# A macaron model's experts stage: the copy of the turned routing weights ahead of the update r, and the transposes of r one unit later

## What is computed

```python
x = x + 0.5 * _L0_ffn_ref(_layernorm(x, axis=-1), ...)
x = x + _L0_attn_ref(_layernorm(x, axis=-1), ...)
x = x + 0.5 * _L0_ffn_ref(_layernorm(x, axis=-1), ...)
x = x + 0.5 * _L1_ffn_ref(_layernorm(x, axis=-1), ...)   # experts, first call
x = x + _L1_attn_ref(_layernorm(x, axis=-1), ...)
x = x + 0.5 * _L1_ffn_ref(_layernorm(x, axis=-1), ...)   # experts, second call
```

```python
xn = (x - mu) * jax.lax.rsqrt(var + EPS) * ln_gamma + ln_beta
abel_out = _gelu(xn @ abel_w + abel_b)
logits = xn @ moe_gate_w + moe_gate_b
topw, topi = jax.lax.top_k(logits, K)
topw = jax.nn.softmax(topw, axis=-1)
w_dense = jnp.sum(jax.nn.one_hot(topi, E, dtype=xn.dtype) * topw[..., None], axis=-2)
h = _gelu(jnp.einsum('bsd,edh->ebsh', xn, ew1) + eb1[:, None, None, :])
eo = jnp.einsum('ebsh,ehd->ebsd', h, ew2) + eb2[:, None, None, :]
moe_out = jnp.einsum('ebsd,bse->bsd', eo, w_dense)
for i in range(NROT):
    moe_out = moe_out @ expm(gens[i])
combined = jnp.concatenate([abel_out, moe_out], axis=-1)
gate = jax.nn.sigmoid(combined @ gc_w + gc_b)
mixed = abel_out * (1.0 - gate) + moe_out * gate
return residual + mixed
```

## Time and profile before

| what | value |
|---|---|
| median of 3 runs | 1009.28 us |
| lowest and highest | 1007.32 and 1010.31 us |
| the profiled execution | 1007.76 us |
| its span in the trace | 1006.0 us |
| PE busy | 859.9 us |
| DVE busy | 711.1 us |
| ACT busy | 638.6 us |
| POOL busy | 604.4 us |
| unit-by-unit work of call one, first product of unit 0 to the last unit's | 313 to 529 us |
| the same of call two | 779 to 992 us |

### The profile page before, as it was taken

The page is one execution under the profiler, slowest core; times in us unless marked ns, Lnnn a source line. Parts: engine busy times, 40 slices in busy tenths (PEclk is TensorE's granted clock), DMA queues, the critical chain, the costliest instruction groups (busy, mean ns, idle before and its releaser), DMA issues.

```text
span 1006.0 us, 14102 instructions
## 1 busy us (share of the span) xinstructions
PE 859.9 (85%) x3862; PEld 460.3 (46%) x3862; DVE 711.1 (71%) x1535; ACT 638.6 (63%) x1153; POOL 604.4 (60%) x610
## 2 busy tenths in 40 slices
PE   7879677767975999999996688888886899999997
PEld 6734333354432444444443355555543344444443
DVE  6945469965563878887863277777786787887774
ACT  3167489967755887778783444444322787778884
POOL 2064675667458766666675254444457766667674
PEclk9999788869997999999997799999997999999999
DMA  8000000000002222211120000000000213223320
GB/s 213 11 1 0 0 0 1 1 1 1 1 0 85 84 86 85 79 48 58 69 84 0 1 1 0 1 1 1 1 1 1 101 69 95 94 94 95 94 95 22
DMA packets 27406, 42.10 MB, mean 42 GB/s; under 512 B 5320, under 2 KB 19036, under 8 KB 27356
## 3 DMA queue, kind: packets, MB, share of 16 engines
q1 hardware_dynamic: 27356, 41.52, 13.0%
HBM read 39.15 MB, written 2.36 MB: 41 GB/s over the span
## 4 chain that ended last, share of the span: by engine, by line
PE 35%; issue 22%; DVE 19%; POOL 14%; ACT 9%; SPq 1%; DVEq 0%; POOLq 0%; DMA 0%; ACTq 0%
PE bank L1478 7%; PE bank L1480 7%; PE bank L1479 7%; POOL arena L810 5%; POOL arena L754 4%; PE bank L1708 3%; DVE arena L1324 3%; ACT bank L1001 3%; POOL rstd L712 2%; DVE arena L1367 1%; DVE arena L1366 1%; DVE stats L1173 1%; PE bank L1678 1%; ACT arena L993 1%; PE bank L1715 1%
## 5 line engine op out<-in xcount | busy, mean ns | idle before, releaser
L790 POOL TENSOR_TENSOR arena<-arena 128x512 f16<-128x512 f32 x256 | 295.3, 1166 | 125.3 <-ACT arena L993 123.5
L1324 DVE TENSOR_TENSOR arena<-bank,arena 128x512 f32<-128x512 f32 x256 | 172.5, 685 | 79.6 <-ACT bank L1001 63.3
L993 ACT ACTIVATE arena<-arena 128x512 f16<-128x512 f32 x256 | 160.8, 628 | 73.8 <-DVE arena L1324 73.7
L1001 ACT ACTIVATE bank<-bank,eb 128x512 f32<-128x512 f32 x256 | 166.8, 656 | 18.9 <-PE bank L1480 18.5
L817 POOL TENSOR_TENSOR arena<-arena 128x512 f32<-128x512 f32 (+1 forms) x24 | 32.7, 1371 | 117.2 <-DVE arena L1442 89.9
L1478 PE MATMUL bank<-arena,ew1hi 128*128 128x512 f16 x256 | 98.5, 385 | 2.0 <-DVE arena L1324 2.0
L1479 PE MATMUL bank<-arena,ew1hi 128*128 128x512 f16 x256 | 98.5, 385 | 0.0
L1480 PE MATMUL bank<-arena,ew1lo 128*128 128x512 f16 x256 | 97.9, 382 | 0.0
L1478 PE MATMUL bank<-arena,ew2hi 128*128 128x512 f16 x256 | 97.3, 380 | 0.1
L1479 PE MATMUL bank<-arena,ew2hi 128*128 128x512 f16 x256 | 97.3, 380 | 0.0
L1480 PE MATMUL bank<-arena,ew2lo 128*128 128x512 f16 x256 | 97.3, 380 | 0.0
(11 more groups left out here) (274 smaller groups left out, 1876.2 us busy)
## 6 DMA issues: line engine op xcount, KB each, us to landing
arena<-wrows SPq DMA_DIRECT2D x64, 512.0 KB, 5.4
X<-in_L_attn_x_dram SPq DMA_DIRECT2D x8, 256.0 KB, 4.3
out_dram<-X SPq DMA_DIRECT2D x8, 256.0 KB, 6.7
arena<-in_L_ffn_ew_dram SPq DMA_DIRECT2D x2, 512.0 KB, 6.4
arena<-in_L_ffn_ew_dram SPq DMA_DIRECT2D x1, 1024.0 KB
wrows<-arena SPq DMA_DIRECT2D x16, 16.0 KB
arena<-in_L_ffn_gens_dram SPq DMA_DIRECT2D x1, 192.0 KB, 2.7
arena<-in_L_ffn_w_gate_dram SPq DMA_DIRECT2D x1, 192.0 KB, 2.9
```

The lines of the kernel that those rows point to most:

```text
L790: pool.tensor_tensor(mo.hlo[:, u % 8, :], mo.hw[:, u % 4, :], mo.hhi[:, u % 8, :], ALU.subtract).then_inc(S.hlo, 1)
L993: A(mo.hhi[:, u % 8, :], mo.hw[:, u % 4, :], ACT.Copy).then_inc(S.hhi, 1)
L1001: A(bank[MM1_BANK[u]][:, :], bank[MM1_BANK[u]][:, :], ACT.Gelu, scale=1.0 / WS, bias=eb1[:, u:u + 1]).then_inc(S.gelu, 1)
L1324: TT(mo.hw[:, u % 4, :], bank[MM1_BANK[u]][:, :], mo.wB[:, p, u // EB, :], ALU.mult)\
```

## The change

On DVE, the copy wT moves from the end of unit 10 to the place right behind the unit-10 product, ahead of m and r. On PE, the transposes of r move from unit 12 to unit 13, that is behind abel and behind the unit-13 first product and the second product beside it. The addition to X stays where it is. Nothing else is changed; ACT, POOL and SP have the same lists.

```diff
@@ experts, VectorE
+                        if lead and u == 10:
+                            dve.wait_ge(S.wpT, i + 2)
+                            after(dve, S.wd, 16 * i)
+                            dve.tensor_copy(mo.wT[0:E, n, :], bank[7][0:E, :]).then_inc(S.wT, 1)
                         if lag and u == 10:
 
                             dve.wait_ge(S.tg, i)
...
-                        if lead and u == 10:
-                            dve.wait_ge(S.wpT, i + 2)
-                            after(dve, S.wd, 16 * i)
-                            dve.tensor_copy(mo.wT[0:E, n, :], bank[7][0:E, :]).then_inc(S.wT, 1)
                 pipeline(dve, first, NCH, step)
@@ experts, TensorE
-                        if lag and u == 12:
+                        if lag and u == 13:
                             pe.wait_ge(S.r, i)
```

## The result

| | before | changed |
|---|---|---|
| median of 4 runs each | 1009.79 us | 1002.90 us |
| lowest and highest | 1007.32 and 1010.81 us | 1001.92 and 1003.03 us |
| ratio, 95% interval | | 0.9935 (0.9919 to 0.9950) |
| profiled execution, its span | 1007.76, 1006.0 us | 1002.81, 1001.1 us |
| first product of a call to the last transposes of r, both calls | 448.83 us | 441.37 us |

The change is 6.9 us faster in the medians. The forecast was 8.8 us faster, 1000.5 us: right sign, 2.4 us off. The time lies 0.4 us outside the narrower range that was given (998.5 to 1002.5) and inside the wider one (996.5 to 1005.5). The two calls give 7.46 us by the traces.

What follows compares the result with a forecast made beforehand. PE, busy 26.38 us of each 27.2 to 27.3 us step, was held about 0.9 us by r. Terms 0.37 + 5.8 + 1.8 + 0.8 = 8.8 us off 1009.28 gave 1000.5 us; range 998.5 to 1002.5, wider 996.5 to 1005.5.

Steps and rivals of the forecast that it cites:

- first period of call one: First step-to-step period of call one: xn slack at the gate logits only 0.42 us, worth 0.37 us.
- four other steady periods of call one: Call one's part of the nine steady periods, each 0.64 us shorter, capped by PE's wait for xn.
- five steady periods of call two: Call two's part of the nine steady periods, each 0.64 us shorter, capped by PE's wait for xn.
- two periods from step 6 to step 7: No next chunk is led in, so no wait for xn: PE keeps its whole 0.89 us, twice.
- two tails: End of each call: r transposes and last second product wait less, 0.4 us each, bounds 0.1 and 0.45.
- The copy ahead of m and r: On DVE, copy starts about 0.6 us after the unit-10 product; PE waits 0.30 us at abel instead of 1.04.
- The transposes behind unit 13: On PE, they wait for nothing, cost 0.44 us, with 1.5 us of cover before L1210; PE gains 0.89 a step.
- What is late next: Gate logits (L1678) wait for xn: PE comes forward 0.64 us, not 0.89; the other 0.25 becomes a new wait.
- DVE, ACT and POOL keep their order and distance from unit 10 to xn: Argument against the slower rival: these engines' sequence and spacing from unit 10 to xn stay unchanged.
- The slower rival: POOL's lock catches DVE's tile updates at units 11 and 12, 0.9 us each: 1022 us; chance 0.06.
- one of them caught: Case of the slower rival where POOL delays only one of the two tile updates: 1011 us, within the noise.
- Less slack downstream: Rival: xn leaves PE only 0.42 us, each period gives 0.37, the tails nothing: 1004.9 us; chance 0.13.

Runs made afterwards that it cites:

- the two half changes: Against the kernel before, only the copy wT ahead of m and r (1015.67 us), or only the transposes of r at unit 13 (1014.14 us).
- moving the logits: Changed kernel with the gate logits on PE, and their wait for xn, at unit 4 instead of unit 3: 997.95 us.
- taking the wait for the copy away: Changed kernel with the abel product behind unit 13's first product and the transposes of r at unit 14: 1001.17 us.
- the copy alone: Changed kernel with the transposes of r back at unit 12, the copy wT still ahead of m and r: 1015.67 us.
- the transposes alone: Kernel before with the transposes of r at unit 13, the copy wT still behind r: 1014.14 us.
- Moving the tile update: Changed kernel with tile updates behind units 8, 11, 14, 15 instead of 8, 11, 12, 14: 1001.85 us.

## Why the prediction was right, and where it was off

| term | forecast | traced |
|---|---|---|
| first period of call one | 0.37 | 0.05 |
| four other steady periods of call one | 2.56 | 1.53 |
| five steady periods of call two | 3.20 | 3.16 |
| two periods from step 6 to step 7 | 1.8 | 1.80 |
| two tails | 0.8 | 0.79 |
| sum | 8.8 | 7.3 (7.46 for the whole calls) |

- **The copy ahead of m and r.** Right: 0.60 behind the product, abel 0.06 behind its end, PE's wait 0.28 for 0.30.
- **The transposes behind unit 13.** Right: no wait, and cover of 1.8 us for 1.5. Both halves are needed, which the two half changes show.
- **What is late next.** Right in mechanism, by two tests: moving the logits makes the periods shorter, and taking the wait for the copy away only lengthens that for xn (in call one that for the tokens too). Its size, 0.64 a period, holds in call two: 0.60 to 0.68.
- **The tails and the last period.** Right, each within 0.1.
- **The sum was mis-sized in one place: the steady periods of call one**, forecast at 2.93 and traced at 1.58. The step of the prediction that failed is "DVE, ACT and POOL keep their order and distance from unit 10 to xn". They keep their order, but DVE reaches the tile update of unit 12 about 0.012 us earlier (3.976 to 3.979 behind the unit-10 product, for 3.986 to 3.991), because the unit-11 product starts 0.012 sooner with r ahead of it than with the copy. The POOL subtraction starts at 3.946 to 3.949 in both, so the update now stands 0.03 behind its start and not 0.04: it takes 1.21 us in all twelve updates of steps 1 to 6 where eight of twelve took 0.33. It goes by DVE's order and not PE's: the copy alone has it in twelve of twelve, the transposes alone have three of twelve at 0.33. The unit-13 product is then 0.24 late (5.11 for 4.87). In call one it carries on through the units 14 and 15 to xn, which ends at 13.48 to 13.69 in steps 2 to 5 where it ended at 13.43 to 13.46. In call two DVE's second wait for ACT takes it up ahead of the unit-14 product. Moving the tile update gave back 1.07 of the 1.35 missing, 0.24 of it in the first period; the remaining 0.28 has no cause shown.
- **The slower rival** named this very mechanism ("one of them caught"). It was priced at 0.9 a period, the whole excess of a caught update. It cost about 0.2 where it was felt, since DVE without it waits 0.77 for ACT at that place, and nothing where a second wait followed. An excess of 0.88 reached PE in full, by the estimate above, only in the runs with m and r behind unit 11.
- **Less slack downstream** came in call one's first period only. It gained 0.05 for 0.37; 0.24 of the difference is the collision, so with the tile update moved it is 0.29.
- **For the slower rival a row was read wrongly.** "Start just as a POOL subtraction ends" holds for the update of unit 11. The one of unit 12 starts 0.04 behind the start of the next subtraction, and in four of its twelve steps it was caught already in the kernel before. Here is a free one and a caught one:

```profile
393.31 1.38 POOL L790 TENSOR_TENSOR arena<-arena 128x512 f16<-128x512 f32 x1 [0.72 <-ACT arena L993]
393.35 0.33 DVE L1337 TENSOR_SCALAR X<-X,keep,shift  x1
...
856.93 1.23 POOL L790 TENSOR_TENSOR arena<-arena 128x512 f16<-128x512 f32 x1 [0.73 <-ACT arena L993]
856.97 1.26 DVE L1337 TENSOR_SCALAR X<-X,keep,shift  x1
```

So the collision was in the trace before; a count of L1337's lengths at unit 12 would have shown it.

## What to carry to other kernels

When a wait on the busiest engine is closed, the gain in a loop is the slack of the next wait around it: read the distance from the releaser's end to the waiting instruction, cap the gain by it, and look whether that second wait can be moved too, since here it was worth half as much again. An operation moved ahead of another only passes its own length on, so check who waits for each of the two, and change both sides together. Where VectorE has small SBUF operations beside GpSimd's, note for each whether it starts inside a GpSimd one, over all steps and not in one, and look what waits stand behind it: they decide whether the collision costs anything.

## What the hardware did that was not expected

**Which of the two waits can turn on a hundredth of a microsecond.** The tile updates L1337 of steps 1 to 6, in all fourteen traces, by how far they start behind a POOL subtraction (1.15 to 1.17 us long where it is not disturbed):

| start behind POOL's start, us | updates | of these at 0.33 |
|---|---|---|
| 0.016 to 0.033 | 175 | 0 |
| 0.037 to 0.043 | 37 | 18 |
| 0.10 to 0.80 | 244 | 0 |
| 0.90 to 1.10 | 146 | 146 |

A caught update ends 0.07 to 0.09 us behind the subtraction, whenever it started, so the later it starts the less it is lengthened (1.22 at 0.02, 1.04 at 0.20, 0.46 at 0.78). Between 0.037 and 0.043 about half go first, and then POOL's row is 1.38 us instead of 1.15. This is a narrow band and not an edge: a start of 0.10 is caught again. Inside the band the start does not decide: at 0.041 both come.

The Trainium skill, page "SBUF — State Buffer", section "SBUF: two separate sides", says that VectorE and GpSimd take a shared pair of ports as an exclusive lock for a whole instruction, and that whoever starts first gets it. The first half fits: one of the two is held for the length of the other. The second half does not by the trace's start times: in those eighteen rows VectorE started second and went first. Which event decides, no run here shows.

**The loser need not be the one that is hurt.** POOL's 0.23 us more in those rows cost nothing that a period shows. VectorE's 0.88 more cost nothing either in the kernel before, where PE was late anyway; it cost 0.24 at the next product in the changed kernel, and 0.88 of PE's wait in the run with m and r behind it.
